# Products of the maxima on half of the rows in an AdaLN attention and mixture-of-experts block

## What is computed

```python
h = _layernorm(x) * (1 + ca) + sa
qkv = h @ w_attn
q = qkv[..., :D].reshape(Bv, Tv, H, HEAD_D).transpose(0, 2, 1, 3)
k, v = qkv[..., D:D + HEAD_D], qkv[..., D + HEAD_D:]
att = jnp.einsum('bhqd,bkd->bhqk', q, k) * scale          # causal mask, softmax over keys
y = jnp.einsum('bhqk,bkd->bhqd', att, v)
x = x + ga * (y @ w_proj)
h = _layernorm(x) * (1 + cb) + sb
x = x + gb * ffn(h)     # 16 experts, the best 4 of a token by sigmoid(h @ gate_w.T), and one shared expert
```

## Time and profile before

| | us |
|---|---|
| median of three runs | 464.36 |
| the profiled execution | 466.41 |
| its span, first to last instruction | 464.6 |

### The profile page before, as it was taken

The page is one execution under the profiler, slowest core; times in us unless marked ns, Lnnn a source line. Parts: engine busy times, 40 slices in busy tenths (PEclk is TensorE's granted clock), DMA queues, the critical chain, the costliest instruction groups (busy, mean ns, idle before and its releaser), DMA issues.

```text
span 464.6 us, 5985 instructions
## 1 busy us (share of the span) xinstructions
PE 388.6 (84%) x2025; PEld 172.2 (37%) x2025; DVE 270.6 (58%) x635; ACT 227.0 (49%) x417; POOL 148.4 (32%) x252
## 2 busy tenths in 40 slices
PE   3666597888799897688789999889999998975996
PEld 2233232433235434133236343323543442224642
DVE  4539366577667785667446784688878711113352
ACT  1320355465466764235345653566676564752400
POOL 4443384626630049622206130014108220202000
PEclk9875589798999999799899999999999999995999
DMA  4241240002000350012520000000052000000000
GB/s 137 39 71 28 49 106 2 2 24 48 1 1 1 83 104 1 2 31 36 129 57 2 23 3 0 23 2 1 1 132 54 2 1 0 24 0 1 1 0 23
DMA packets 16413, 14.45 MB, mean 31 GB/s; under 512 B 5824, under 2 KB 11600, under 8 KB 16384
## 3 DMA queue, kind: packets, MB, share of 16 engines
q1 hardware_dynamic: 15968, 13.68, 13.8%
q10 hardware_dynamic: 416, 0.39, 0.3%
HBM read 9.65 MB, written 1.15 MB: 23 GB/s over the span
## 4 chain that ended last, share of the span: by engine, by line
PE 64%; DVE 14%; POOL 6%; ACT 6%; issue 3%; DMA 3%; SPq 2%; ACTq 0%; POOLq 0%; DVEq 0%
PE bank L836 60%; DVE mn L751 6%; POOL xn L456 3%; ACT pr L598 2%; SPq L392 2%; DMA qa<-shiftT 2%; PE bank L984 2%; POOL pr L540 1%; POOL rstd L447 1%; PE bank L866 1%; DVE sl L823 1%; DMA xs<-in_L_attn_x 1%; ACT L598 1%; DVE q_left L713 1%; ACT hT L562 1%
## 5 line engine op out<-in xcount | busy, mean ns | idle before, releaser
L751 DVE TENSOR_REDUCE mn<-bank 128x1 f32<-128x512 f32 (+6 forms) x304 | 179.4, 627 | 84.2 <-PE bank L836 83.7
L598 ACT ACTIVATE pr<-bank 128x512 f32<-128x512 f32 x288 | 159.3, 598 | 109.9 <-PE bank L836 108.6
L836 PE MATMUL bank<-qa,ka 100*128 100x512 bf16 x288 | 112.4, 399 | 17.3 <-DMA qa<-shiftT 12.8
L836 PE MATMUL bank<-ka,qa 96*128 96x512 bf16 (+7 forms) x384 | 114.0, 341 | 13.5 <-DVE mn L751 12.1
L540 POOL TENSOR_SCALAR_AFFINE_SELECT pr<-pr 128x256 f32<-128x256 f32 x128 | 48.9, 422 | 190.2 <-ACT pr L598 190.1
L836 PE MATMUL bank<-pr,va 128*32 128x512 f32 x576 | 81.4, 638 | 3.8 <-POOL pr L540 3.6
L836 PE MATMUL bank<-hT_parts,up_parts 128*128 128x512 f32 x216 | 67.7, 439 | 1.8 <-DVE sl L823 1.7
L836 PEld LDWEIGHTS bank<-qa,ka 100*128 100x128 bf16 x288 | 28.5, 102 | 102.9 <-ACT pr L598 37.6
L836 PEld LDWEIGHTS bank<-ka,qa 96*128 96x128 bf16 x384 | 36.2, 103 | 48.9 <-DVE mn L751 26.2
L836 PEld LDWEIGHTS bank<-hT_parts,up_parts 128*128 128x128 f32 x216 | 39.7, 196 | 19.2 <-issue 8.8
L836 PE MATMUL bank<-tri,onehot 128*128 128x64 bf16 (+2 forms) x176 | 38.8, 221 | 0.0
(11 more groups left out here) (132 smaller groups left out, 283.4 us busy)
## 6 DMA issues: line engine op xcount, KB each, us to landing
comb_wide<-comb_rows SPq DMA_DIRECT2D x6, 1024.0 KB, 9.8
qa<-qp SPq DMA_DIRECT2D x48, 64.0 KB
xs<-in_L_attn_x SPq DMA_DIRECT2D x4, 256.0 KB, 5.6
qa<-shiftT SPq DMA_DIRECT2D x64, 2.0 KB
out_x<-res SPq DMA_DIRECT2D x4, 256.0 KB, 2.2
sl<-in_L_ffn_e_win SPq DMA_DIRECT2D x1, 512.0 KB, 3.8
sl<-in_L_ffn_e_vin SPq DMA_DIRECT2D x1, 512.0 KB, 5.5
w_out<-in_L_ffn_e_wout SPq DMA_DIRECT2D x1, 512.0 KB, 5.5
```

The source lines that it names most:

```text
L598: act.activation(pr[:, n % NPB, g, :], s_bank[in_s[x] % NS][:, :], ACT.Exp, scale=SCALE).then_inc(s_read, 1)
L751: v.tensor_reduce(mn[:, place[u] % 2, part, hf, a, r:r + n], m_bank[k % NM][:, 0:n * w].rearrange("p (n w) -> p n w", w=w), AX.X, ALU.max, ...
L836: return pe.matmul(out, lhsT, rhs, start=start, stop=stop, skip_group_check=True)
```

## The change

The rows are laid out anew. Half 1 begins at row 64 (`Q`) instead of 48, in qa, k_all, ka and wk. Behind each half's 48 rows come its own two rows of shifts (48, 49 and 112, 113), and scores contract over 114 rows. Rows 50 to 63 of qa hold nothing, so VectorE clears rows 32 to 63 of qa in its first instruction, and SP waits for that ahead of its DMAs. `k_all` is kept for all tokens. A job of maxima contracts over the 48 rows of its half only, of qa with k_all instead of ka, starting at partition 0 or 64, and its mask over 64 rows. Scores still read ka. Row masks on GpSimd take two instructions instead of six. The result of a chunk is written over xs instead of into `res`. The plan is unchanged.

```diff
-    MROWS, SROWS = 2 * KROWS, 2 * KROWS + 4
+    SROWS = Q + KROWS + 2
...
-        k_all = sb("k_all", [P, CH], bf16)
+        k_all = sb("k_all", [P, B, T], bf16)
...
-        res = sb("res", [P, 2, 4, D], f32)
...
                     sp.wait_ge(q_hi, 2 * q_no[c] + 2)
+                    sp.wait_ge(qa_cleared, 1)
...
-                                    r = KROWS * hf + n * HD
+                                    r = Q * hf + n * HD
...
-                            r, s = MROWS + 2 * hf, 8 * (2 * hf + a)
+                            r, s = Q * hf + KROWS, 8 * (2 * hf + a)
...
-                    sp.dma_start(ov[:, 4 * c:4 * c + 4, :], res[:, turn_of[c] % 2, :, :]).then_inc(out_sent[c], 16)
+                    sp.dma_start(ov[:, 4 * c:4 * c + 4, :], xs[:, 4 * c:4 * c + 4, :]).then_inc(out_sent[c], 16)
...
-                        own(gp.tensor_scalar(in_group[:, 2:3], rowno[:, :], float(MROWS), None, ALU.is_ge))
-                        own(gp.tensor_scalar(in_group[:, 3:4], rowno[:, :], float(MROWS + 2), None, ALU.is_lt))
-                        own(gp.tensor_tensor(in_group[:, 2:3], in_group[:, 2:3], in_group[:, 3:4], ALU.mult))
-                        own(gp.tensor_scalar(in_group[:, 3:4], rowno[:, :], float(KROWS), None, ALU.is_lt))
-                        own(gp.tensor_tensor(in_group[:, 0:1], in_group[:, 2:3], in_group[:, 3:4], ALU.add))
-                        gp.tensor_scalar(in_group[:, 1:2], in_group[:, 0:1], -1.0, 1.0, ALU.mult, ALU.add
-                                         ).then_inc(rows_ready, 1)
+                        gp.tensor_scalar(in_group[:, 0:1], rowno[:, :], float(KROWS + 2), None, ALU.is_lt)
+                        gp.tensor_scalar(in_group[:, 1:2], rowno[:, :], float(Q), None, ALU.is_ge).then_inc(rows_ready, 1)
...
-                    gp.wait_ge(k_done, q_no[c])
-                    gp.tensor_tensor(k_all[:, :], k_rest[:, :], k_mid_part[:, :], ALU.subtract).then_inc(k_left, 1)
+                    b, t0 = c // CB, c % CB * CH
+                    gp.tensor_tensor(k_all[:, b, t0:t0 + CH], k_rest[:, :], k_mid_part[:, :], ALU.subtract).then_inc(k_left, 1)
...
+            v.memset(qa[32:64, :, :, :], 0.0).then_inc(qa_cleared, 1)
             for x in plan:
...
                     v.wait_ge(small_ready[at[x]], use[x] + 1)
-                    if p >= 2:
-                        v.wait_ge(out_sent[CHUNKS[p - 2]], 16)
-                    v.tensor_tensor(res[:, p % 2, :, :], small[at[x]][:, :].rearrange("p (t d) -> p t d", d=D),
+                    v.tensor_tensor(xs[:, 4 * c:4 * c + 4, :], small[at[x]][:, :].rearrange("p (t d) -> p t d", d=D),
...
-                        ins = mm(to[:, i, :], qa[0:MROWS, b, r + i, 2 * q0:2 * q0 + 2 * Q],
-                                 ka[0:MROWS, hf, b, k0:k0 + w], stop=not m)
+                        ins = mm(to[:, i, :], qa[Q * hf:Q * hf + KROWS, b, r + i, 2 * q0:2 * q0 + 2 * Q],
+                                 k_all[Q * hf:Q * hf + KROWS, b, k0:k0 + w], stop=not m)
                     if m:
-                        ins = mm(to[:, :, w - Q:w], onehot[:, :, :].rearrange("p q s -> p (q s)"),
-                                 tri[:, :].unsqueeze(1).broadcast_to([P, n, Q]), start=False)
+                        ins = mm(to[:, :, w - Q:w], onehot[Q * hf:Q * hf + Q, :, :].rearrange("p q s -> p (q s)"),
+                                 tri[Q * hf:Q * hf + Q, :].unsqueeze(1).broadcast_to([Q, n, Q]), start=False)
```

More of the change, by code:

```diff
@@ L330, in adaln_attention_moe_kernel @@
         consts, wk_ready, rows_ready, cleared = sem("consts"), sem("wk_ready"), sem("rows_ready"), sem("cleared")
+        qa_cleared = sem("qa_cleared")
         tri_ready, picker_ready = sem("tri_ready"), sem("picker_ready")
@@ L684, in _ @@
                     v.wait_ge(cleared, 1)
-                    v.tensor_copy(wk[:, 0:MROWS].rearrange("p (x d) -> p x d", d=HD),
-                                  w_attn[:, D:D + HD].unsqueeze(1).broadcast_to([P, MROWS // HD, HD])
+                    v.tensor_copy(wk[:, :].rearrange("p (f x d) -> p f x d", f=2, d=HD)[:, :, 0:len(PRODUCTS), :],
+                                  w_attn[:, D:D + HD].unsqueeze(1).unsqueeze(1).broadcast_to([P, 2, len(PRODUCTS), HD])
                                   ).then_inc(wk_ready, 1)
@@ L690, in _ @@
                     v.tensor_scalar(mod[:, 1, :], mod[:, 1, :], 1.0, None, ALU.add).then_inc(small_read[at[x]], 1)
-                    v.wait_ge(rows_ready, 2)
+                    v.wait_ge(rows_ready, 3)
+                    own(v.tensor_scalar(has_mid[:, :], rowno[:, :], float(Q), -float(Q), ALU.is_ge, ALU.mult))
+                    own(v.tensor_tensor(rowno[:, :], rowno[:, :], has_mid[:, :], ALU.add))
                     v.tensor_scalar(onehot[:, :, :], colno[:, :, :], rowno[:, 0:1], None, ALU.is_equal)
                     v.tensor_scalar(tri[:, :], colno[:, :, 0], rowno[:, 0:1], LOW, ALU.is_gt, ALU.mult).then_inc(tri_ready, 1)
[L694 to L697, removed]
                     v.tensor_scalar(has_mid[:, :], rowno[:, :], float(MID_ROWS), None, ALU.is_lt)
@@ L730, in _ @@
                     v.wait_ge(k_mid, 1)
-                    v.tensor_tensor(k_all[:, :], k_rest[:, :], k_mid_part[:, :], ALU.subtract).then_inc(k_left, 1)
+                    b, t0 = c0 // CB, c0 % CB * CH
+                    v.tensor_tensor(k_all[:, b, t0:t0 + CH], k_rest[:, :], k_mid_part[:, :], ALU.subtract).then_inc(k_left, 1)
                 elif kind == "k_set":
@@ L736, in _ @@
                     for hf in range(2):
-                        ins = v.tensor_scalar(ka[:, hf, b, t0:t0 + CH], k_all[:, :], in_group[:, hf:hf + 1], None, ALU.mult)
+                        ins = v.tensor_scalar(ka[:, hf, b, t0:t0 + CH], k_all[:, b, t0:t0 + CH], in_group[:, hf:hf + 1], None, ALU.mult)
                     ins.then_inc(k_done, 1)
@@ L825, in _ @@
                     c = x[1]
-                    p = turn_of[c]
                     v.wait_ge(small_ready[at[x]], use[x] + 1)
-                    if p >= 2:
-                        v.wait_ge(out_sent[CHUNKS[p - 2]], 16)
-                    v.tensor_tensor(res[:, p % 2, :, :], small[at[x]][:, :].rearrange("p (t d) -> p t d", d=D),
+                    v.tensor_tensor(xs[:, 4 * c:4 * c + 4, :], small[at[x]][:, :].rearrange("p (t d) -> p t d", d=D),
                                     xs[:, 4 * c:4 * c + 4, :], ALU.add).then_inc(small_read[at[x]], 1)
```

## The result

The changed kernel takes 514.66 us (median of four executions: 513.04, 513.15, 516.17 and 1204.64 us; 513.15 for the first three), the kernel before 464.05 us in the same rounds. The ratio is 1.1032, 95% interval 1.0986 to 1.1079. Executions more than 1.5% above the fastest of their kernel, like the one at 1204.64 us, are left out of all ratios and of the medians of the experiments. The profiled one took 513.15 us, its span is 511.4.

The account below looks back on a forecast made before the run. The prediction took TensorE to bound the middle stretch. To the span of 464.6 us it added 42 for the maxima's changes and 13.5 for the clearing, 520.1, and forecast 520 us, range 484 to 536.

Parts of the forecast that it names:

- The bound: Steady block of the middle stretch: TensorE has no gap, so work added there lengthens the block, 3.29 to about 4.05 us.
- The price of a change: Between full-height operations and half-height maxima on TensorE: each of 463 added changes of array division costs 0.095 us, 44 us.
- The step from picker's 16 rows to 48 rows: Row division's price for the maxima was read from picker, the kernel's one existing case: 0.09 us on the way in.
- Changes on the path: Middle stretch: of 51 us added to TensorE, 37 plus 7 lie on the path; less 2 for pairs, 42 us.
- Weights no longer covered: Behind 86 of the changes on TensorE, the next f32 weights lose their cover: 0.08 us each, 7 us.
- rival D: Half-height matmuls lose the covered weight load, 0.095 us for 190 second matmuls: 18 us more, 538 us; chance 0.07.
- The 27 pairs: Adjacent maxima jobs in the middle can run side by side: at most 5.9 us gained, 2 us taken.
- The clearing: VectorE's new first instruction, clearing rows 32 to 63 of qa, makes start-up 13.5 us later.
- Rival A: The clearing goes by four-byte words or faster, ends at 9.5 us, start-up 4.8 us late: 511 us; chance 0.22.
- Edits at nothing: Fewer row masks, k_all per chunk, results in xs, SP's new wait and the DMAs into qa: no time.
- B: The changes hide behind waits for ScalarE or VectorE and only the clearing is seen: 478 us; chance 0.08.
- C: Not slower: row division costs nothing, the 27 pairs give 5.9 us, the clearing costs 1.2: 460 us; chance 0.05.

Follow-up runs that it names:

- the third experiment: Changed kernel with the clearing of qa in four pieces: 512.38 us; with the pieces placed anew, all in idle time of VectorE, 510.30 us, ratio 1.0951.
- The half dose: Changed kernel with only the maxima jobs of half 0 at half height, those of half 1 at full height: 487.08 us, ratio 1.0432.
- the first experiment: Changed kernel with the maxima's matmuls and their mask back at full height, layout and clearing kept: 471.49 us, ratio 1.0081 to the kernel before.

## Why the prediction was right, and where it was off

**The bound** (TensorE paces the middle): right. TensorE has no gap in the steady block and lengthens it one for one; the prediction made 3.29 to about 4.05 us, measured 3.28 to 4.04.

**The price of a change**: right, 0.10 us measured in the steady block where 0.095 was taken from pv and picker. Its count, 463, is the plan's and was not counted again in the trace. The step from picker's 16 rows to 48 rows held.

**Changes on the path**: the sum came out, 43.0 us measured for 42, but its parts did not, so that the agreement to 1 us is luck. I let the lower clock cost 3 us at most, in the bounds. In the middle stretch the granted clock fell from 0.94 to 0.89, that is (twice what it lacks of 1, times 320 and 361 us) from 38 to 79 us at 1.2 GHz. At the 0.29 to 0.39 us of the third experiment, 41 us more are 12 to 16 us. A second reading: of the 57 blocks from pv to pv that hold maxima, 42 run at 2.4 GHz throughout in both kernels, and they grew from 212.7 to 235.9 us, 10.9%. The other 15 grew from 95.3 to 114.7, 9 us more than by the same share. So, by these two estimates, 27 to 34 us come from the changes themselves, 53 to 67% of their 51 us, and 9 to 16 us from the clock. The step that I mis-sized is the share on the path, 86% by my sum (37 + 7 of 51). The half dose fits this: its clock in the middle was 0.93, and it cost less per change. Why the clock falls with more changes stays open, and nothing was run that holds it fixed. A want of work on TensorE is not seen: in the changed kernel's stretch from 128 to 163 us TensorE shows as busy for 33.54 of 35.00 us, and the granted clock there is 0.76.

**Weights no longer covered**: behind a maximum the transposes of osb have 0.49 us to the next score instead of 0.44 (355.83 to 356.32), 0.05 where I took 0.08. For bf16 weights and on one half, zero was right; rival D falls.

**The 27 pairs**: small as said. They do run side by side.

**The clearing**: this is the step that failed. I took 13.5 us, at one bf16 value per step, from GpSimd's memsets as the nearest rows. Measured are 4.7 us: 8192 words, done at 9.4 us. Rival A had this term to 0.1 us (9.5 and 4.8). The rate per step was right, 1.04 ns for 1.06; the number of steps was not, 8192 for 16384. The sentence of the Trainium skill, VectorE: DVE Perf Modes, section on zero memsets, that a bf16 memset of zero may be issued as half as many 32-bit words holds here. GpSimd's rows could not tell them apart, since all of them that I used write f32. Against the median of 514.66 us the forecast's 520 is 5.3 too high and rival A's 511 is 3.7 too low; against the three executions' 513.15 they are 6.9 and 2.2 off. The measured time lies between the two, and nearer to rival A, which had 0.22. Executions of the changed kernel, at clocks of 0.880 and 0.887, are 3.1 us apart.

**Edits at nothing**: confirmed to within 1 us by the first experiment, whose middle is 0.9 us above that of before and whose start is the clearing's.

**Rivals B and C** fall by the steady block. C's point was right in one thing: side by side is worth 0.21 us a pair, once the plan makes pairs.

## What to carry to other kernels

Dividing TensorE's array by rows pays only if the divided matmuls stand next to each other in its order of work; count the places where the shape changes, at 0.1 us each, before the pairs that gain 0.21. Here 463 such places, with the lower clock that went with them, cost 43 of 464 us, and grouping in pairs, without touching a matmul, gave these back. A clearing needs no place on the path: put it, in pieces, where its engine waits, and look at what stands behind each piece.

## What the runs showed that I had not expected

- Frequent changes of shape go with a lower granted clock: 0.923 before, 0.887 after, 0.92 with full height back. It also differs between executions of one kernel: 0.898 to 0.865 in the six of the changed kernel with its clearing in the gaps, 0.929 to 0.916 in the 17 of the kernel before in the same rounds. That changes of shape cause it is not shown.
- A memset of 16384 bf16 zeros shows as 8192 uint32, at 1.04 ns a word from start to start, while its row is 0.86 ns a word long (1.76 us for 2048).
- Bunching the maxima at two places of a block costs some 9 us, at half and at full height alike.
